# Inverse roots by log and exp on ScalarE, the softmax maximum subtracted on VectorE, and new engine orders in a six-layer local transformer

## The chip, the cores and the metric

The program runs on one core of one Trainium2 chip. The metric is the device time of one execution in microseconds (us); lower is better. PE is TensorE, PEld its weight loads, DVE VectorE, ACT ScalarE, POOL GpSimd, SP SyncE.

## The reference, cut to what matters

Sixteen sequences of 256 tokens, 128 wide, in float32, go through a delta-rule mixer and then through six layers of a local transformer. The layers are what the change touches. Per layer and sequence:

```python
qkv = x @ Wqkv                       # 16 heads of 64; half of x is shifted by one token first
q = l2norm(q) * qs;  k = l2norm(k) * ksc      # t / max(norm(t), 1e-12)
q = q*cos*scale + rotate_half(q)*sin*scale    # k the same with 1/scale
sim = q @ k^T * 8, masked to the token's window of 32 and the one before
attn = softmax(sim)
x = x + (attn @ v) @ Wo
mu, var = mean(x), mean((x - mu)**2)          # on x shifted again
xn = (x - mu) / sqrt(var + 1e-5) * g + b
a, gate = split(xn @ W1 + b1)
x = x + (a * gelu(gate)) @ W2 + b2
```

Two things matter below: the 1/sqrt of 64 sums of squares and 2 variances per token (128 x 66 numbers per item), and the softmax over 64 keys, computed as exp(sim - max) divided by its sum.

## The kernel before

normalise_input, delta_mixer and write_output frame the program and stay as they are. The work of interest is local_transformer. It is a software pipeline: pipeline(body) calls each engine's body once per *item* (one sequence in one layer, 96 items, 100 bodies with the ends). In one body five items are in flight at different stages: new (projected and rotated), turn (scaled, transposed, its values projected), att (scored, softmax), out (weighted sum, output projection) and ffn. Each engine has its own list of calls, written by hand, and runs them strictly in that order; engines meet only through counting semaphores (need(engine, semaphore, value) is a wait that stands in front of the next instruction).

An item has 8 chunks of queries and keys (128 tokens x 512 columns) and 4 units of scores (half a sequence, half of the heads). The steps and their engines:

- query_key (PE, L1416, three matmuls per chunk) fills the single bank ps_proj. rotate (DVE, L1255 and L1262) writes rot_a and rot_b, add (POOL, L1000) adds them into qk, square (ACT, L1079) and sum_squares (DVE, L1270) give the sums ss. The next query_key waits for square.
- inverse_roots (DVE, L1310, L1313, then newton_rsqrt, L63 to L71, eleven steps on 128 x 66) makes rn from ss. scale (POOL, L1010) multiplies qk by rn; turn_qk (PE, L1451) transposes it; turned_out (ACT, L1090) copies it to qT or kT. spread (PE, L1560), deviate (DVE, L1326) and affine (ACT, L1161) use rn for the layer norm.
- score (PE, L1462 and L1468) fills a bank with mask and products; top (DVE, L1279) takes the negated maximum; shift (PE, L1478) adds it in the same bank by a matmul; exp (ACT, L1111) writes pr; total (DVE, L1287, L1290); norm (POOL, L1019); turn_probs (PE, L1492) transposes into the bank ps_p; probs_out (ACT, L1120) copies it to pT; weigh (PE, L1508) multiplies with the values; heads_taken, turn_heads, heads_out and join_heads (L1535) follow.
- value (PE, L1416) projects values, one quarter at a time, into the same bank ps_p, which it shares with turn_probs; value_out (ACT, L1102) copies a quarter to v. window (SP, L947) then copies v into vw, in the layout that weigh wants: 14 DMAs for the first half of an item, 16 for the second. vw has three slots, so the DMAs of the second half wait for weigh(att,1) of the same body (semaphore valued) and for value_out(turn,3). value_out(turn,0) of the next body overwrites v and so waits until all DMAs of both halves have landed.
- ffn_in (PE, L1576, three parts), gelu (ACT, L1170), hidden (DVE, L1335), ffn_out (PE, L1585), layer_out (DVE, L1343).

ps_p makes this order in each body: value(turn,0), its copy, turn_probs(out,3), its copy probs_out(out,3), value(turn,1), its copy, turn_probs(att,0), and so on.

Of the kernel before, what the change touches and what calls it, by code (L numbers as in the profile page):

```python
# [15 lines left out]
P = 128  # L16
# [15 lines left out]
NPREP = 9  # L32
# [14 lines left out]
NEWTON = 11  # L47

# [754 lines left out]
def local_transformer(nc, stateT, ident, wqkv_d, scales_d, wb_d, par_d, rot_d, mask_d):  # L803
# [8 lines left out]
    with ExitStack() as stack:  # L812
        def sb(name, shape, dt=F32):
# [18 lines left out]
        ident_r = sb("ident_r", [P, P], F32R)  # L832
# [11 lines left out]
        rn_t = sb("rn_t", [P, NNORM + 2])  # L844
        qT = sb("qT", [P, 2, NPAIR, L])
# [4 lines left out]
        negmax = sb("negmax", [P, 2, NPAIR], F32R)  # L850
# [18 lines left out]
            "ss_floored", "rn_steps", "added", "scaled", "turned", "turned_out", "v_projected", "v_out",  # L869
# [97 lines left out]
        def _(pool):  # L967
# [8 lines left out]
            nc.gpsimd.tensor_copy(ident_r[:, :], ident[:, :]).then_inc(S["prepared"], 1)  # L976
# [26 lines left out]
            def scale(x, c):  # L1003

                if not x.there:
                    return
                need(pool, S["rn_steps"], x.u * NEWTON + NEWTON)
# [14 lines left out]
            def body(b):  # L1022
                new, turn, att, out, ffn = b.items
                if turn.there:
                    low_half(new, "added", turn.u * 8 + 7)
                else:
                    low_half(new, "prepared", NPREP)
                add(turn, 7)
                scale(turn, 0)
                scale(turn, 1)  # L1030
                scale(turn, 2)
                add(new, 0)
                add(new, 1)
                norm(out, 3)
                scale(turn, 3)
                add(new, 2)
                norm(att, 0)
                scale(turn, 4)
                add(new, 3)
                scale(turn, 5)  # L1040
                add(new, 4)
                norm(att, 1)
                scale(turn, 6)
# [3 lines left out]
                add(new, 6)  # L1047
# [4 lines left out]
        def _(act):  # L1052
# [52 lines left out]
            def exp(x, k):  # L1105
# [4 lines left out]
                need(act, S["p_turned"], x.u * 4 + (k - 1))  # L1110
                nc.scalar.activation(pr[:, k % 2, :, :].rearrange("p h n -> p (h n)"), ps_s[k % 2][:, :], ACT.Exp)\  # L1111
# [51 lines left out]

            def gelu(x):
# [4 lines left out]
                for c, bank in enumerate((ps_c[:, 0:L], ps_c[:, L:2 * L], ps_g[:, 0:L])):  # L1169
                    nc.scalar.activation(gate[:, c, :], bank, ACT.Gelu, bias=par[:, FCH + c:FCH + c + 1])\  # L1170
                        .then_inc(S["gelu_done"], 1)

            def body(b):
# [4 lines left out]
                if b.switch == 1:  # L1178
# [3 lines left out]
                        .then_inc(S["conv_act"], 1)  # L1182
                if b.switch == -1:
                    convert(b, (4, 5), (S["v_projected"], turn.u * 4))
                exp(out, 3)
                probs_out(out, 2)
                heads_taken(out, 1)
                heads_out(out, 1)
                turned_out(att, 7)
                exp(att, 0)  # L1190
                square(new, 0)
                turned_out(turn, 0)
                affine(ffn)
                heads_taken(out, 2)
# [5 lines left out]
                square(new, 2)  # L1200
                probs_out(out, 3)
                turned_out(turn, 3)
                exp(att, 1)
                value_out(turn, att, 1)
                square(new, 3)
                heads_taken(out, 3)
                probs_out(att, 0)
                heads_out(out, 2)
                exp(att, 2)
                turned_out(turn, 4)  # L1210
                square(new, 4)
                heads_out(out, 3)
                heads_taken(att, 0)
                turned_out(turn, 5)
# [5 lines left out]
                square(new, 5)  # L1220
                shift_state(out)
                square(new, 6)
                square_centred(out)
                probs_out(att, 1)
                heads_out(att, 0)
                square(new, 7)
                turned_out(turn, 6)
                value_out(turn, att, 3)

            pipeline(body)  # L1230

        @block.vector
        def _(dve):
# [39 lines left out]
            def top(x, k):  # L1273

                if not x.there:
                    return
                need(dve, S["scored"], x.u * 4 + (k + 1))
                need(dve, S["shifted"], x.u * 4 + (k - 1))
                nc.vector.tensor_reduce(negmax[:, k % 2, :], ps_s[k % 2][:, :].rearrange("p (h n) -> p h n", h=NPAIR),  # L1279
                                        AX.X, ALU.max, negate=True).then_inc(S["maxed"], 1)  # L1280

# [24 lines left out]
            def inverse_roots(new, out):  # L1306
# [7 lines left out]
                if new.there:  # L1314
                    need(dve, S["ss_floored"], new.u + 1)
                if out.there:
                    need(dve, S["var_eps"], out.u + 1)
                if new.there or out.there:
                    newton_rsqrt(nc, dve, ss[:, :], rn[:, new.q, :], rn_t[:, :], S["rn_steps"], new.u * NEWTON)
# [26 lines left out]
            def body(b):  # L1346
                new, turn, att, out, ffn = b.items
                if b.switch == -2:
# [7 lines left out]
                    need(dve, S["rot_ready"], b.layer + 1)  # L1356
                if b.switch == -1:
                    convert(b, (4, 5), 4)
                rotate(new, 0, 0)
                rotate(new, 0, 1)  # L1360
                top(att, 1)
                deviate(ffn)
                sum_squares(new, 0)
                rotate(new, 1, 0)
                rotate(new, 1, 1)
                total(out, 3)
                rotate(new, 2, 0)
                rotate(new, 2, 1)
                top(att, 2)
                sum_squares(new, 1)  # L1370
                hidden(ffn)
                sum_squares(new, 2)
                total(att, 0)
                rotate(new, 3, 0)
                rotate(new, 3, 1)
                sum_squares(new, 3)
                rotate(new, 4, 0)
                rotate(new, 4, 1)
                layer_out(ffn)
# [6 lines left out]
                total(att, 1)  # L1386
# [3 lines left out]
                total(att, 2)  # L1390
# [398 lines left out]
```

## Time and profile before

| | us |
|---|---|
| runs shown | 4334.82, 4339.76, 4342.02 |
| median | 4339.76 |
| profiled execution | 4339.03 |
| its span, first to last instruction | 4336.7 |
| the 96 items of the transformer, by the start of the first and of the last spread matmul | 873.2 to 4305.5 |

The profile lists an instruction with its start and duration. Matmuls overlap: the next may start before the former's shown end, so what one costs PE is read from start to start. "Idle before" is the time that the engine stood still, with the instruction that ended it. The granted TensorE clock is at its full level through the whole transformer.

### The profile page before, as it was taken

Reading aid. Unit: us, or ns where it says so; the run is one execution under the profiler, and the core shown is the slowest. Engines: PE = TensorE matmul, PEld = TensorE weight load, DVE = VectorE, ACT = ScalarE, POOL = GpSimd, SP = SyncE. Lnnn points to the kernel's source line nnn. Section 1 sums busy time; section 2 is a strip of 40 time slices with the busy share of each in tenths; the row PEclk is TensorE's granted clock in tenths of the full one; section 3 lists DMA queues with packets and bytes.
Section 4 is the critical chain, followed back from the end, with each engine's and each line's share of the span. In section 5 each row is a group of like instructions: output and inputs, shape, how many; then the busy total and the mean of one; then the engine's idle time right before and its main releaser. Section 6 shows DMA issues by size and latency. Waiting matters only on the chain. (4 is left out here: it accounts for less than half of the span.)

```text
span 4336.7 us, 147276 instructions
## 1 busy us (share of the span) xinstructions
PE 3870.3 (89%) x60944; PEld 3124.7 (72%) x60944; DVE 3287.5 (76%) x6184; ACT 2662.9 (61%) x4807; POOL 2311.6 (53%) x2140
## 2 busy tenths in 40 slices
PE   4747652799999999999999999999999999999996
PEld 4635541577787777778778777787777777877775
DVE  4385566788888888888888888888888888888873
ACT  2322211477777777777777677777677776777773
POOL 0000001566666666666666666666666666666661
PEclk9666655799999999999999999999999999999998
DMA  1000000222222222223222222222222222222222
GB/s 58 22 12 12 2 12 24 57 73 57 57 57 67 72 57 57 57 51 84 57 56 58 54 66 72 57 57 57 61 78 57 57 57 55 67 57 56 57 57 59
DMA packets 155311, 231.93 MB, mean 53 GB/s; under 512 B 48144, under 2 KB 58128, under 8 KB 152976
## 3 DMA queue, kind: packets, MB, share of 16 engines
q1 hardware_dynamic: 154640, 222.41, 19.7%
q8 instruction: 492, 8.06, 0.8%
q14 instruction: 179, 1.47, 0.1%
HBM read 29.28 MB, written 4.19 MB: 8 GB/s over the span
## 5 line engine op out<-in xcount | busy, mean ns | idle before, releaser
L1000 POOL TENSOR_TENSOR qk<-rot_a,rot_b 128x512 f32<-128x512 f32 x768 | 985.4, 1283 | 754.0 <-PE bank L1451 535.6
L1010 POOL TENSOR_TENSOR qk<-qk,rn 128x512 f32<-128x512 f32 x768 | 806.0, 1060 | 132.9 <-DVE rn L71 132.9
L1255 DVE TENSOR_TENSOR rot_a<-bank,rot 128x512 f32<-128x512 f32 x768 | 526.4, 685 | 373.6 <-PE bank L1416 363.1
L1079 ACT ACTIVATE sq<-bank 128x512 f32<-128x512 f32 x768 | 463.2, 603 | 418.5 <-DVE rot_b L1262 390.5
L1416 PE MATMUL bank<-w_hi,xs_hi 128*128 128x512 f32 x1152 | 565.5, 491 | 60.2 <-ACT sq L1079 36.1
L1270 DVE TENSOR_REDUCE ss<-sq 128x8 f32<-128x512 f32 x768 | 513.8, 669 | 132.4 <-ACT sq L1079 132.2
L1019 POOL TENSOR_TENSOR pr<-pr,prec 128x512 f32<-128x512 f32 x384 | 400.9, 1044 | 322.0 <-DVE prec L1290 322.0
L1262 DVE TENSOR_TENSOR rot_b<-bank,rot 128x512 f32<-128x512 f32 x768 | 522.3, 680 | 0.0
L1451 PE MATMUL bank<-ident,qk 128*128 128x128 f32 x3072 | 470.3, 276 | 25.4 <-POOL qk L1010 21.8
L1416 PE MATMUL bank<-w_hi,xs_lo 128*128 128x512 f32 x1152 | 459.7, 399 | 0.0
L1416 PE MATMUL bank<-w_lo,xs_hi 128*128 128x512 f32 x1152 | 459.2, 399 | 0.0
L1451 PEld LDWEIGHTS bank<-ident,qk 128*128 128x128 f32 x3072 | 373.1, 141 | 114.4 <-POOL qk L1010 39.5
L1468 PEld LDWEIGHTS bank<-kT,qT 64*32 64x32 f32 x24576 | 362.8, 108 | 88.6 <-issue 88.6
L1468 PE MATMUL bank<-kT,qT 64*32 64x64 f32 x24576 | 425.3, 219 | 0.0
L1508 PE MATMUL bank<-vw,pT 128*32 128x128 f32 x12288 | 417.5, 277 | 1.2 <-ACT pT L1120 1.2
L1508 PEld LDWEIGHTS bank<-vw,pT 128*32 128x32 f32 x12288 | 313.9, 110 | 90.0 <-issue 86.5
L1535 PE MATMUL bank<-oT,wo 128*128 128x256 f32 x1536 | 347.3, 379 | 1.4 <-ACT oT L1137 1.4
L1535 PEld LDWEIGHTS bank<-oT,wo 128*128 128x128 f32 x1536 | 291.4, 190 | 44.7 <-ACT oT L1137 1.8
L1137 ACT ACTIVATE oT<-bank 128x512 f32<-128x512 f32 x384 | 229.7, 598 | 106.5 <-PE bank L1523 101.0
L1416 PEld LDWEIGHTS bank<-w_hi,xs_hi 128*128 128x128 f32 x1152 | 221.0, 192 | 94.3 <-issue 38.2
L1576 PE MATMUL bank<-xn,w 128*128 128x256 f32 x1152 | 282.2, 381 | 5.5 <-ACT xn L1161 3.4
L1102 ACT ACTIVATE v<-bank 128x512 f32<-128x512 f32 x384 | 228.6, 595 | 85.8 <-DMA vw<-v 60.9
(242 smaller groups left out, 7377.3 us busy)
## 6 DMA issues: line engine op xcount, KB each, us to landing
vw<-v SPq DMA_DIRECT2D x2880, 64.0 KB, 2.0
stage<-in_wqkv SPq DMA_DIRECT2D x6, 1536.0 KB, 6.3
stage<-in_wb_all SPq DMA_DIRECT2D x6, 1088.0 KB, 5.4
d_band<-in_band SPq DMA_DIRECT2D x8, 512.0 KB, 5.6
d_xt<-in_x SPq DMA_DIRECT2D x4, 512.0 KB, 4.1
base_scratch<-d_res SPq DMA_DIRECT2D x4, 512.0 KB, 2.8
o_base<-base_scratch SPq DMA_DIRECT2D x1, 2048.0 KB, 8.0
out<-o_base SPq DMA_DIRECT2D x4, 512.0 KB, 3.3
```

The costliest lines, as they stand in the source:

```text
L1000: nc.gpsimd.tensor_tensor(qk[:, c, :], rot_a[:, c % 2, :], rot_b[:, c % 2, :], ALU.add)\
L1010: nc.gpsimd.tensor_tensor(y, y, rn[:, x.q, 8 * c:8 * c + 8].unsqueeze(2).to_broadcast([P, 8, DH]), ALU.mult).then_inc(S["scaled"], 1)
L1019: nc.gpsimd.tensor_tensor(y, y, prec[:, k % 2, :].unsqueeze(2).to_broadcast([P, NPAIR, KEYS]), ALU.mult).then_inc(S["normed"], 1)
L1079: nc.scalar.activation(sq[:, :], ps_proj[:, :], ACT.Square).then_inc(S["squared"], 1)
L1255: nc.vector.tensor_tensor(rot_a[:, c % 2, :].rearrange("p (h d) -> p h d", h=8), ps_proj[:, :].rearrange("p (h d) -> p h d", h=8), cos, AL ...
L1262: nc.vector.tensor_tensor(rot_b[:, c % 2, :].rearrange("p (h a d) -> p h a d", h=8, a=2), y[:, :, ::-1, :], sin, ALU.mult).then_inc(S["rot ...
L1270: nc.vector.tensor_reduce(ss[:, 8 * c:8 * c + 8], sq[:, :].rearrange("p (h d) -> p h d", h=8), AX.X, ALU.add).then_inc(S["summed"], 1)
L1416: mm = nc.tensor.matmul(out[:, :], x[:, q, half * P:(half + 1) * P], w[:, cols:cols + CK], start=n == 0, stop=n == 2)
L1451: mm = nc.tensor.transpose(ps_turn[:, i * P:(i + 1) * P], qk[:, c, i * P:(i + 1) * P], ident[:, :])
L1468: mm = nc.tensor.matmul(bank[w * WIN:(w + 1) * WIN, h * KEYS:(h + 1) * KEYS], qT[rows, x.q, h, q0:q0 + WIN], kT[rows, x.q, h, q0:q0 + KEYS ...
L1508: mm = nc.tensor.matmul(ps_o[w * WIN:(w + 1) * WIN, c * P:(c + 1) * P].rearrange("p (r d) -> p r d", r=2), pT[:, k % 2, c, w * WIN:(w + 1) ...
L1535: mm = nc.tensor.matmul(ps_c[:, 0:L], wo[:, c, :], oT[:, c, :], start=c == 0, stop=c == NPAIR - 1)
```

## The change

- The shift matmul, its float32r identity and its semaphore wait in top go. A new DVE step, shift, adds the negated maximum to the bank and writes pr; exp then runs on pr in place.
- newton_rsqrt goes from the transformer (it stays in the other stages). floors (DVE) is what is left of inverse_roots; roots (ACT) takes Ln of ss into ss_log and Exp of -0.5 times that into rn; polish (DVE) makes one Newton step of three instructions.
- After the Gelus the table set with both Exp and Ln is loaded ahead of its first use (EXP_LN_TABLE).
- The lists of PE, DVE, ACT and POOL are written in another order. SP's is unchanged.

```diff
             def exp(x, k):
                 need(act, S["shifted"], x.u * 4 + (k + 1))
-                need(act, S["p_turned"], x.u * 4 + (k - 1))
-                nc.scalar.activation(pr[:, k % 2, :, :].rearrange("p h n -> p (h n)"), ps_s[k % 2][:, :], ACT.Exp)\
+                y = pr[:, k % 2, :, :].rearrange("p h n -> p (h n)")
+                nc.scalar.activation(y, y, ACT.Exp)\
                     .then_inc(S["exped"], 1)
...
+            def roots(new, out):
+                if new.there:
+                    need(act, S["ss_floored"], new.u + 1)
+                if out.there:
+                    need(act, S["var_eps"], out.u + 1)
+                if not new.there and not out.there:
+                    return
+                nc.scalar.activation(ss_log[:, :], ss[:, :], ACT.Ln).then_inc(S["logged"], 1)
+                need(act, S["logged"], new.u + 1)
+                need(act, S["scaled"], min(new.u - 1, NSEQ * DEPTH) * 8)
+                need(act, S["rstd_spread"], out.u - 1)
+                nc.scalar.activation(rn[:, new.q, :], ss_log[:, :], ACT.Exp, scale=-0.5).then_inc(S["rooted"], 1)
...
                         .then_inc(S["gelu_done"], 1)
+                nc.scalar.preload_act_table_set(EXP_LN_TABLE)
...
+                value_out(turn, att, 0)
                 gelu(ffn)
-                value_out(turn, att, 0)
...
+            def shift(x, k):
+                need(dve, S["maxed"], x.u * 4 + (k + 1))
+                need(dve, S["p_turned"], x.u * 4 + (k - 1))
+                nc.vector.tensor_tensor(pr[:, k % 2, :, :], ps_s[k % 2][:, :].rearrange("p (h n) -> p h n", h=NPAIR),
+                                        negmax[:, k % 2, :].unsqueeze(2).to_broadcast([P, NPAIR, KEYS]), ALU.add)\
+                    .then_inc(S["shifted"], 1)
...
+            def polish(new, out):
+                n, y = new.u * POLISH, rn[:, new.q, :]
+                need(dve, S["rooted"], new.u + 1)
+                nc.vector.tensor_tensor(rn_t[:, :], y, y, ALU.mult).then_inc(S["rn_steps"], 1)
+                need(dve, S["rn_steps"], n + 1)
+                nc.vector.scalar_tensor_tensor(rn_t[:, :], rn_t[:, :], -0.5, ss[:, :], ALU.mult, ALU.mult).then_inc(S["rn_steps"], 1)
+                need(dve, S["rn_steps"], n + 2)
+                nc.vector.scalar_tensor_tensor(y, rn_t[:, :], 1.5, y, ALU.add, ALU.mult).then_inc(S["rn_steps"], 1)
...
-            def shift(x, k):
-                need(pe, S["maxed"], x.u * 4 + (k + 1))
-                nc.tensor.matmul(ps_s[k % 2][:, :].rearrange("p (h n) -> p h n", h=NPAIR), ident_r[:, :],
-                                 negmax[:, k % 2, :].unsqueeze(2).to_broadcast([P, NPAIR, KEYS]),
-                                 start=False, stop=True, skip_group_check=True).then_inc(S["shifted"], 1)
```

The new order at three places. First ACT, in the middle of an ordinary body, around the Gelus of ffn. Before (L1079 is square, L1102 value_out, L1120 probs_out, L1090 turned_out, L1111 exp, L1170 gelu):

```order
L1079 ACTIVATE sq<-bank 128x512 [waits t_summed,t_rotated]
L1170 ACT_TABLE_LOAD
L1170 ACTIVATE gate<-bank,par 128x256 [waits t_c_mm]
L1170 ACTIVATE gate<-bank,par 128x256 x2
L1102 ACTIVATE v<-bank 128x512 [waits t_vw_in0,t_vw_in2,t_v_projected]
L1090 ACTIVATE qT<-bank 128x4x128 [waits t_turned]
L1079 ACTIVATE sq<-bank 128x512 [waits t_summed,t_rotated]
L1120 ACTIVATE pT<-bank 128x512 [waits t_valued,t_p_turned]
L1090 ACTIVATE kT<-bank 128x4x128 [waits t_turned]
L1111 ACT_TABLE_LOAD [waits t_p_turned]
L1111 ACTIVATE pr<-bank 128x512 [waits t_shifted]
```

With the change, the same place (L1082 is square, L1105 value_out, L1187 gelu, L1189 the load ahead, L1123 probs_out):

```order
L1082 ACTIVATE sq<-bank 128x512 [waits t_summed,t_rotated]
L1105 ACTIVATE v<-bank 128x512 [waits t_vw_in0,t_vw_in2,t_v_projected]
L1187 ACT_TABLE_LOAD
L1187 ACTIVATE gate<-bank,par 128x256 [waits t_c_mm]
L1187 ACTIVATE gate<-bank,par 128x256 x2
L1189 ACT_TABLE_LOAD
L1123 ACTIVATE pT<-bank 128x512 [waits t_valued,t_p_turned]
L1082 ACTIVATE sq<-bank 128x512 [waits t_summed,t_rotated]
L1093 ACTIVATE qT<-bank 128x4x128 [waits t_turned]
L1105 ACTIVATE v<-bank 128x512 [waits t_v_projected]
```

The copy of the first value quarter, which waits for the landing of vw (t_vw_in), has moved from behind the Gelus to in front of them, and the second table load from behind probs_out(out,3) to in front of it.

Second PE, at the same place. Before (L1478 is shift, L1576 ffn_in part 2, L1492 turn_probs, L1451 turn_qk, L1416 query_key or value, L1585 ffn_out; a row "x3" is the rest of a group):

```order
L1478 MATMUL bank<-negmax,ident_r 128x512 [waits t_maxed]
L1576 MATMUL bank<-xn,w 128x256 [waits t_gelu_done,t_xn_ready]
L1576 MATMUL bank<-xn,w 128x256
L1492 MATMUL bank<-ident,pr 128x128 [waits t_v_out,t_normed]
L1492 MATMUL bank<-ident,pr 128x128 x3
L1451 MATMUL bank<-ident,qk 128x128 [waits t_turned_out,t_scaled]
L1451 MATMUL bank<-ident,qk 128x128 x3
L1478 MATMUL bank<-negmax,ident_r 128x512 [waits t_maxed]
L1416 MATMUL bank<-w_hi,xs_hi 128x512 [waits t_squared]
...
L1585 MATMUL bank<-gate,w 128x256 [waits t_hid_done]
L1585 MATMUL bank<-gate,w 128x256 x2
L1416 MATMUL bank<-w_hi,xs_hi 128x512 [waits t_p_turned_out]
```

With the change (L1523 is turn_probs, L1607 ffn_in part 2, L1456 value and then query_key, L1539 weigh):

```order
L1523 MATMUL bank<-ident,pr 128x128 [waits t_v_out,t_normed]
L1523 MATMUL bank<-ident,pr 128x128 x3
L1607 MATMUL bank<-xn,w 128x256 [waits t_gelu_done,t_xn_ready]
L1607 MATMUL bank<-xn,w 128x256
L1456 MATMUL bank<-w_hi,xs_hi 128x512 [waits t_p_turned_out]
L1456 MATMUL bank<-w_hi,xs_lo 128x512
L1456 MATMUL bank<-w_lo,xs_hi 128x512
L1456 MATMUL bank<-w_hi,xs_hi 128x512 [waits t_squared]
L1456 MATMUL bank<-w_hi,xs_lo 128x512
L1456 MATMUL bank<-w_lo,xs_hi 128x512
L1539 MATMUL bank<-vw,pT 32x128 [waits t_o_out,t_p_turned_out]
```

ffn_in part 2 has moved behind turn_probs(out,3), value(turn,1) ahead of query_key 3 and of ffn_out, and both shifts are gone.

Third DVE, at the boundary of two bodies, with the change (before, eleven rows L63 to L71 stood between L1313 and rotate; L1339 and L1342 are floors, L1275 and L1282 rotate, L1350 to L1354 polish, L1298 top, L1361 deviate, L1307 shift):

```order
L1339 TENSOR_SCALAR ss<-ss 128x64 [waits t_summed]
L1342 TENSOR_SCALAR ss<-bank 128x2 [waits t_var_done]
L1275 TENSOR_TENSOR rot_a<-bank,rot 128x512 [waits t_added,t_projected]
L1350 TENSOR_TENSOR rn_t<-rn 128x66 [waits t_rooted]
L1352 SCALAR_TENSOR_TENSOR rn_t<-rn_t,ss 128x66 [waits t_rn_steps]
L1354 SCALAR_TENSOR_TENSOR rn<-rn_t,rn 128x66 [waits t_rn_steps]
L1282 TENSOR_TENSOR rot_b<-bank,rot 128x512
L1298 TENSOR_REDUCE negmax<-bank 128x8 [waits t_scored]
L1361 TENSOR_TENSOR xc<-xc,bank 128x256 [waits t_rstd_spread]
L1307 TENSOR_TENSOR pr<-bank,negmax 128x512 [waits t_p_turned,t_maxed]
```

The roots now end inside the first rotate of the next body. On PE the boundary has changed too: weigh(att,1) is followed by score(turn,0), turn_probs(att,2), and in the next body by query_key 0, turn_qk 7, score(att,1) and turn_heads(out,1), which stood elsewhere; value(turn,3)'s copy, value_out(att,3) by the names of the next body, is ACT's first work after high_half there, where before it was the last of the former body.

## Rows read from the trace of the kernel before

**Rows 1.** The page, part 1: busy time, share of the span, instructions.

```profile
PE 3870.3 (89%) x60944; PEld 3124.7 (72%) x60944; DVE 3287.5 (76%) x6184; ACT 2662.9 (61%) x4807; POOL 2311.6 (53%) x2140
```

**Rows 2.** Waits: PE from 1000 to 4300 us, ACT and SP whole span.

```profile
PE bank L1492 <- ACT v L1102: 23.4, 30, 1.8
...
ACT v L1102 <- DMA vw<-v: 60.9, 61, 4.3
...
SPq L54 <- PE bank L1508: 1498.9, 189, 12.6
```

**Rows 3.** All spread matmuls (L1560): duration min/median/max, first and last start.

```profile
L1560 PE MATMUL bank<-ident,rn x384: 274/275/582, 873.2 to 4305.5; 128*128 128x128 f32 x192
```

**Rows 4.** PE's timeline: start us, us, instruction, [idle before <-releaser].

```profile
2034.74 1.08 PE L1508 MATMUL bank<-vw,pT 128*32 128x128 f32 x32
...
2070.43 1.08 PE L1508 MATMUL bank<-vw,pT 128*32 128x128 f32 x32
2071.45 0.48 PE L1478 MATMUL bank<-negmax,ident_r 128*128 128x512 f32 x1
2071.77 0.60 PE L1451 MATMUL bank<-ident,qk 128*128 128x128 f32 x4
2072.20 0.60 PE L1492 MATMUL bank<-ident,pr 128*128 128x128 f32 x4
2072.56 0.46 PE L1478 MATMUL bank<-negmax,ident_r 128*128 128x512 f32 x1
2072.86 0.39 PE L1462 MATMUL bank<-mask,ident_b 128*128 128x512 bf16 x1
...
2074.21 0.66 PE L1523 MATMUL bank<-ident,o_tok 128*128 128x128 f32 x4
2074.62 0.48 PE L1416 MATMUL bank<-w_hi,xs_hi 128*128 128x512 f32 x1
...
2077.45 0.66 PE L1451 MATMUL bank<-ident,qk 128*128 128x128 f32 x4 [0.24 <-POOL qk L1010]
...
2086.13 0.63 PE L1492 MATMUL bank<-ident,pr 128*128 128x128 f32 x4 [0.80 <-ACT v L1102]
...
2087.30 0.41 PE L1416 MATMUL bank<-w_hi,xs_hi 128*128 128x512 f32 x1
...
2088.01 1.46 PE L1585 MATMUL bank<-gate,w 128*128 128x256 f32 x6
2089.11 0.58 PE L1416 MATMUL bank<-w_hi,xs_hi 128*128 128x512 f32 x1
...
2107.20 1.08 PE L1508 MATMUL bank<-vw,pT 128*32 128x128 f32 x32
```

**Rows 5.** ACT's timeline, the stretch around the Gelus, and the next body's copy.

```profile
2080.86 0.60 ACT L1079 ACTIVATE sq<-bank 128x512 f32<-128x512 f32 x1 [0.29 <-DVE rot_b L1262]
2081.48 1.28 ACT L1170 ACT_TABLE_LOAD   x1
2082.77 1.20 ACT L1170 ACTIVATE gate<-bank,par 128x256 f32<-128x256 f32 x3
2085.39 0.60 ACT L1102 ACTIVATE v<-bank 128x512 f32<-128x512 f32 x1 [1.41 <-DMA vw<-v]
...
2120.95 0.60 ACT L1102 ACTIVATE v<-bank 128x512 f32<-128x512 f32 x1 [0.21 <-DMA vw<-v]
```

**Rows 6.** SP's timeline, the second half's DMAs of one item; landing times of line L947.

```profile
2071.62 10.68 SPq L947 DMA_DIRECT2D vw<-v  x16
...
DMA to landing us min/median/max: 1.9/2.0/3.8
```

**Rows 7.** DVE's timeline, the root steps between two bodies: first, longest, and rotate.

```profile
2070.81 0.87 DVE L63 TENSOR_SCALAR rn_t<-ss 128x66 int32<-128x66 int32 x1
...
2073.64 1.32 DVE L67 TENSOR_TENSOR rn_t<-rn 128x66 f32<-128x66 f32 x1
...
2076.20 0.68 DVE L1255 TENSOR_TENSOR rot_a<-bank,rot 128x512 f32<-128x512 f32 x1
```

More of the change, by code:

```diff
@@ L1032, in body @@
                 add(new, 0)
+                norm(out, 3)
                 add(new, 1)
[L1034 removed]
+                norm(att, 0)
+                add(new, 2)
                 scale(turn, 3)
[L1036 to L1037 removed]
                 scale(turn, 4)
+                scale(turn, 5)
                 add(new, 3)
[L1040 removed]
+                scale(turn, 6)
                 add(new, 4)
                 norm(att, 1)
[L1043 removed]
                 add(new, 5)
@@ L1219, in body @@
                         .then_inc(S["conv_act"], 1)
-                square(new, 5)
                 shift_state(out)
                 square(new, 6)
+                probs_out(att, 1)
+                turned_out(turn, 6)
                 square_centred(out)
[L1224 to L1228, printed above, removed]
+            nc.scalar.preload_act_table_set(EXP_LN_TABLE)
             pipeline(body)
@@ L1356, in body @@
                     need(dve, S["rot_ready"], b.layer + 1)
+                rotate(new, 0, 0)
+                polish(turn, ffn)
+                rotate(new, 0, 1)
                 if b.switch == -1:
                     convert(b, (4, 5), 4)
-                rotate(new, 0, 0)
-                rotate(new, 0, 1)
-                top(att, 1)
+                top(att, 0)
                 deviate(ffn)
+                shift(att, 0)
                 sum_squares(new, 0)
@@ L1378, in body @@
                 rotate(new, 4, 1)
+                shift(att, 2)
                 layer_out(ffn)
@@ L1401, in body @@
                 rotate(new, 7, 1)
-                top(turn, 0)
+                top(att, 3)
+                shift(att, 3)
                 sum_squares(new, 7)
-                inverse_roots(new, out)
+                floors(new, out)
             pipeline(body)
@@ L1590, in body @@
                 query_key(b, new, 0)
+                turn_qk(att, 7)
+                score(att, 1)
+                turn_heads(out, 1)
                 weigh(out, 2)
@@ L1593, in body @@
                 turn_qk(turn, 0)
+                query_key(b, new, 1)
+                turn_heads(out, 2)
                 value(b, turn, 0)
-                query_key(b, new, 1)
                 turn_qk(turn, 1)
@@ L1598, in body @@
                 ffn_in(ffn, 1)
+                query_key(b, new, 2)
                 turn_qk(turn, 2)
-                query_key(b, new, 2)
                 score(att, 2)
-                shift(att, 1)
+                turn_probs(out, 3, turn, 0)
                 ffn_in(ffn, 2)
-                turn_probs(out, 3, turn, 0)
-                turn_qk(turn, 3)
-                shift(att, 2)
-                query_key(b, new, 3)
-                ffn_out(ffn)
-                value(b, turn, 1)
-                weigh(out, 3)
-                turn_heads(out, 2)
-                turn_probs(att, 0, turn, 1)
+                value(b, turn, 1)
+                query_key(b, new, 3)
+                weigh(out, 3)
+                turn_probs(att, 0, turn, 1)
+                ffn_out(ffn)
+                turn_qk(turn, 3)
+                turn_heads(out, 3)
                 query_key(b, new, 4)
@@ L1615, in body @@
                 weigh(att, 0)
-                turn_heads(out, 3)
+                turn_qk(turn, 5)
                 value(b, turn, 2)
-                turn_qk(turn, 5)
                 query_key(b, new, 5)
@@ L1627, in body @@
                 mean(out)
+                turn_qk(turn, 6)
+                query_key(b, new, 7)
+                value(b, turn, 3)
                 turn_heads(att, 0)
-                query_key(b, new, 7)
-                score(turn, 0)
-                value(b, turn, 3)
-                turn_qk(turn, 6)
                 variance(out)
                 weigh(att, 1)
-                shift(att, 3)
-                turn_qk(turn, 7)
+                score(turn, 0)
                 turn_probs(att, 2, turn, 3)
-                shift(turn, 0)
-                score(turn, 1)
-                turn_heads(att, 1)
             pipeline(body)
```

96 lines of the change are left out of this document (50 added, 46 removed).

## Prediction

> **What bounds the kernel now.** The page comes first: TensorE (PE) is 89% busy over the span, and it is the only engine near full [rows 1]. The list of waits inside the transformer comes second. PE's longest wait there is turn_probs (L1492) for ScalarE's copy of the value projection (value_out, L1102), and that copy in turn waits for the DMAs vw<-v. SyncE issues those DMAs and waits, 189 times, for weigh (L1508) [rows 2]. So PE's own stream is the bound, and behind it, nearly as long, stands one ring: weigh on PE, 16 DMAs, a copy on ScalarE, PE again. I read that ring closely, because the change moves two of its members.
>
> A body (one turn of the pipeline, one item) takes (4305.5 - 873.2) / 95 = 36.13 us on average [rows 3]. Let T0 be the end of weigh(att,1). Undisturbed, T0 to T0 is 2070.43 - 2034.74 = 35.69 us; in the next body it is 2107.20 - 2070.43 = 36.77 [rows 4]. The difference is 0.80 us of wait at turn_probs and 0.24 at a transpose.
>
> **The ring before.** T0 = 2070.43 + 1.08 = 2071.51 [rows 4]. SyncE issues at 2071.62, 16 DMAs in 10.68 us, about 0.6 each, so the last starts near 2081.7; it lands 2.0 us later at the median, 3.8 at most [rows 6]. The earliest landing is therefore T0 + 12.2. The copy starts at V = 2085.39 - 2071.51 = T0 + 13.88 after 1.41 us of waiting; in the next body at 2120.95 - 2108.28 = T0 + 12.67 after 0.21 [rows 4, 5]. ScalarE was free at T0 + 12.46 in both. Over the run it waited 61 times, 60.9 us [rows 2], so V was 12.46 + 1.00 = 13.46 in 61 bodies and between 12.2 and 12.46 in the other 35: I take 12.3 there and a mean V of 13.04. From V to turn_probs is 0.74, from there to the next T0 22.15: 13.88 + 0.74 + 22.15 = 36.77, the disturbed body exactly.
>
> **Part 1: the shift matmul leaves PE.** Four per body. From start to start they take 0.32 (2071.45 to 2071.77) and 0.30 (2072.56 to 2072.86) [rows 4], and I take 1.24 us per body; PE's stream falls to 34.45. Their shown duration, 0.48 and 0.46, overlaps the next matmul. The Trainium skill (Perfetto Trace Analysis, Identifying the Most-Contended Engine) calls matmul busy time a bad measure since matmuls are pipelined; by busy time the gain would read 1.9 us per body, and the trace agrees with the skill.
>
> **Part 2: VectorE.** It gains four 128x512 passes from PSUM, each like rotate's (0.68 us) [rows 7], 2.7 us. It loses eight of eleven root steps: the eleven took 2076.20 - 2070.81 = 5.39 us, three remain, between 0.8 us (0.26 each) and 3.9 (if each is held as long as the longest step, 1.32 [rows 7]). The balance is between -1.9 and +1.2 us on an engine with 76% [rows 1]: no bound.
>
> **Part 3: roots on ScalarE.** Two 128x66 activations, for which there is no row; a 128x512 one takes 0.60, so 0.1 to 0.6 each, likely 0.3. They stand behind heads_taken(out,1), which waits for T0, and the polish stands behind rotate(new,0,0). I get roots done near T0 + 2.4, that rotate near T0 + 3.4, polish near T0 + 4.2 (with long steps T0 + 7.3), against T0 + 4.7 now (2076.20) [rows 7]. PE asks for it in spread, near T0 + 5.8. A delay of 1.5 us there would fall inside the stall of part 4, so this costs nothing. The listed order shows two table loads per body, as before: Ln and all Exps run under the one set that is loaded after the Gelus.
>
> **Part 4: the ring after.** ScalarE now does value_out(turn,0) *before* gelu(ffn); before, after it. SyncE's order and the wait for all 16 DMAs are unchanged. Queued behind the waiting copy are now the Gelu table load, three Gelus, the load of the other set, and probs_out(out,3). And PE has moved too: value(turn,1) must wait for probs_out(out,3), as before, but ffn_in(ffn,2), which needs the second Gelu, now comes behind turn_probs. From V on [rows 5]: copy to the load 0.62 (as 2080.86 to 2081.48), load 1.29 (to 2082.77), Gelus 1.21, second load 1.29, probs_out 0.62, wake-up of PE 0.14 (2085.39 + 0.60 to 2086.13) [rows 4, 5]: 5.17 us until value(turn,1) starts. From there to T0: before, 2108.28 - 2089.11 = 19.17. The new order has query_key 3 (2087.30 to 2088.01, 0.71), ffn_out (to 2089.11, 1.10) and one turn_qk (0.43) more in this stretch, and one turn_heads (0.41) and one score (1.35) less [rows 4]: 19.65 us. The ring is V + 24.82 us. PE alone would reach value(turn,1) at 34.45 - 19.65 = T0 + 14.80; the ring lets it start at 13.04 + 5.17 = T0 + 18.21. So 3.4 us of stall per body take the place of the 1.24 us saved.
>
> I followed the other queues along this order with the same durations. Behind value(turn,1) the tightest is the single projection bank (project, two rotates, square: about 3.3 us per chunk against 4.2 between query_key 3 and 4); it has some 0.6 us to spare. GpSimd's adds are late by nothing that PE asks for.
>
> **Sum.** 13.04 + 24.82 = 37.86 us against 36.13, +1.73 x 95 = +164 us. Off this comes what the layer changes hide: 23.4 us of PE's wait for the copy [rows 2] over the 91 bodies between 1000 and 4300 us are 0.26 each, so an ordinary body is 35.69 + 0.26 = 35.95 and (36.13 - 35.95) x 95 = 17 us belong to conversions at layer changes, most of which will lie under the wait for the landing. 4339.0 (the profiled execution, 2.3 more than its span, 0.7 under the median 4339.8) + 164 - 17 = 4486 us.
>
> **Rivals.** (A) Faster: the landing does not hold the copy and PE's stream sets the time. A body is then 34.45 + 0.18: -1.50 x 95 = -143, 4196 us. It needs V below 34.45 - 24.82 = T0 + 9.6; the gain begins below 36.13 - 24.82 = T0 + 11.3. Against it: 16 issues alone take 10.7. For it: no row shows this ring with the new ScalarE order, and I may have misjudged what stands behind the copy. Chance 0.10.
> (B) V near T0 + 11.3, 4340 us: 0.04.
> (C) Slower still: the DMAs start late. Their first needs value_out(att,3) too, which now stands behind high_half in the next body; I get it done at T0 - 0.2. If square_centred, the transposes or the wait for centre push it 1 us past T0, each body is 1 us longer: 4580 us. Chance 0.07.
> (D) Slower, by the table loads. The rows give 1.29 us from a load to the next activation [rows 5], and the sum goes by them; if a load held the engine twice as long on this path, two loads would add 2.6 us per body, 4730 us. Chance 0.02. The Trainium skill (ScalarE: Activation LUTs, What ACT_TABLE_LOAD costs) puts a switch at 2.66 us with the drain; the trace does not agree.
> That the roots or the shift would not be as the diff says I exclude: the listed orders show them.
>
> **How the numbers follow.** The forecast has 0.77. Its own range: with V = 12.2 throughout the body is 37.02, +0.89 x 95 = +85, with 17 to 35 us off 4390; with V 0.5 us later 4535. Range 4385 to 4535; A, B, most of C and D (about 0.2) lie outside. A comparison of this kernel can tell 0.2%, some 9 us, from no change. Faster 0.10, same 0.04, slower 0.86.
>
> **What would show it.** Right: ScalarE's v copy waits 2 to 4 us for vw<-v in nearly every body; the Gelu load starts 0.6 us after it; PE waits at ffn_in (L1607) for the gate about 1.8 us and at value (L1456) for pT about 1.4; T0 to T0 is 37 to 38.5 us; PE's busy share falls though no other engine rises. Wrong: the copy lands before T0 + 11.3, or PE's stalls lie elsewhere (spread, score), or bodies of 34.5 us.

## The result and the profile after

| | before | after |
|---|---|---|
| median, us | 4338.72 (4334.82 to 4342.02) | 4621.19 (4616.26 to 4635.49) |
| ratio to before | | 1.0657 (95% interval 1.063 to 1.0684) |
| profiled execution, us | 4339.03 | 4625.48 |

The kernel is 6.6% slower. The direction was forecast, the size was not: 4625.5 against 4486, and above the range's 4535. The profile says first that no engine took over.

The page, busy time and the granted TensorE clock in 40 slices of the span, answers to [rows 1]:

```profile
PE 3962.5 (86%) x60560; PEld 3173.1 (69%) x60560; DVE 3143.7 (68%) x5776; ACT 2754.4 (60%) x5009; POOL 2296.7 (50%) x2139
...
PEclk9666656999999999999999999999999999999998
```

PE has 384 matmuls fewer and 92 us more busy time, which already says that its instructions became longer. The digit 9 stands for 90% or more and hides a part of the answer; the stretch from 1600 to 2200 us shows it (length, then PE, PEld, DVE, ACT and POOL busy with instruction counts, granted clock, DMA share, GB/s), before first, after second:

```profile
1600.00:2200.00 600.00, 585.27 (x8755) 473.05 (x8745) 485.48 (x928) 428.59 (x780) 392.77 (x363) 1.00 0.24 61
```

```profile
1600.00:2200.00 600.00, 555.81 (x8044) 444.87 (x8043) 426.32 (x797) 408.24 (x751) 358.11 (x333) 0.94 0.23 57
```

Next the spread matmuls of after, as in [rows 3]:

```profile
L1591 PE MATMUL bank<-ident,rn x384: 274/276/583, 867.9 to 4590.3; 128*128 128x128 f32 x192
```

A body takes (4590.3 - 867.9) / 95 = 39.18 us against 36.13, and 3.05 x 95 = 290 us is the whole difference, 4625.5 - 4339.0 = 286.5, within 4 us. So only the transformer's bodies matter.

The waits of after from 1000 to 4500 us (total us, times, longest), as in [rows 2]:

```profile
ACT v L1105 <- DMA vw<-v: 243.2, 83, 4.2
...
PE bank L1607 <- ACT gate L1187: 119.7, 83, 1.5
...
PE bank L1523 <- ACT v L1105: 59.2, 50, 2.0
...
PE bank L1456 <- ACT pT L1123: 46.8, 59, 1.1
```

ScalarE's copy now waits for the landing in 83 bodies, 2.9 us each, and PE has three stalls in the place of one: turn_probs for the copy, ffn_in part 2 for the Gelu, value(turn,1) for probs_out. One body on ScalarE, with T0 = 2050.66 (weigh at 2049.58 plus its 1.08 us), as in [rows 5]:

```profile
2052.90 0.26 ACT L1175 ACTIVATE ss_log<-ss 128x66 f32<-128x66 f32 x1 [0.34 <-DVE ss L1342]
2053.19 0.26 ACT L1179 ACTIVATE rn<-ss_log 128x66 f32<-128x66 f32 x1
...
2064.76 0.60 ACT L1105 ACTIVATE v<-bank 128x512 f32<-128x512 f32 x1 [3.70 <-DMA vw<-v]
2065.37 1.28 ACT L1187 ACT_TABLE_LOAD   x1
2066.67 1.20 ACT L1187 ACTIVATE gate<-bank,par 128x256 f32<-128x256 f32 x3
2067.89 1.28 ACT L1189 ACT_TABLE_LOAD   x1
2069.18 0.60 ACT L1123 ACTIVATE pT<-bank 128x512 f32<-128x512 f32 x1
```

And on PE, the same body and then the next one (T0 = 2090.09), as in [rows 4]:

```profile
2049.58 1.08 PE L1539 MATMUL bank<-vw,pT 128*32 128x128 f32 x32
...
2065.50 0.63 PE L1523 MATMUL bank<-ident,pr 128*128 128x128 f32 x4 [1.45 <-ACT v L1105]
2067.65 1.87 PE L1607 MATMUL bank<-xn,w 128*128 128x256 f32 x4 [1.52 <-ACT gate L1187]
2069.83 0.79 PE L1456 MATMUL bank<-w_hi,xs_hi 128*128 128x512 f32 x1 [0.32 <-ACT pT L1123]
...
2108.99 0.79 PE L1456 MATMUL bank<-w_hi,xs_hi 128*128 128x512 f32 x1
2109.58 0.63 PE L1456 MATMUL bank<-w_hi,xs_lo 128*128 128x512 f32 x1
2110.01 0.63 PE L1456 MATMUL bank<-w_lo,xs_hi 128*128 128x512 f32 x1
2110.44 0.63 PE L1456 MATMUL bank<-w_hi,xs_hi 128*128 128x512 f32 x1
...
2118.66 0.39 PE L1456 MATMUL bank<-w_hi,xs_lo 128*128 128x512 f32 x1
2118.89 0.39 PE L1456 MATMUL bank<-w_lo,xs_hi 128*128 128x512 f32 x1
```

The chain is that of the prediction, with V = 2064.76 - 2050.66 = T0 + 14.10 and 5.07 us from V to value(turn,1). New is what comes then. Behind the stalls the starts of equal 128x512 matmuls lie 0.43 us apart (2109.58 to 2110.01), nine microseconds later 0.23 (2118.66 to 2118.89): PE runs at the lower of its two clocks, 1.2 instead of 2.4 GHz, for a few microseconds in most bodies. The Trainium skill (TensorE: Matmul & The Clock Gate, Back-to-back issue gap) gives N / 1.2 ns for a cold matmul, which at 512 columns is 427 ns, and the trace agrees with its 0.43 us.

The trace of before holds the same thing, in four places before its last bodies. At each of its five layer changes PE stalls 1.84 us. Behind four of these stalls the clock falls (behind the last, at 3638.03, and behind one of 2.56 us that follows it at 3646.22, it does not), so the clock is not at its full level through the whole transformer, as was said above. The first of them:

```profile
1304.66 0.38 PE L1462 MATMUL bank<-mask,ident_b 128*128 128x512 bf16 x1 [1.84 <-ACT pr L1111]
...
1307.08 0.63 PE L1416 MATMUL bank<-w_hi,xs_lo 128*128 128x512 f32 x1
1307.51 0.63 PE L1416 MATMUL bank<-w_lo,xs_hi 128*128 128x512 f32 x1
```

The spacing is 0.43 us here too. In before it came four times in 96 bodies; with the change it comes in most of them.

I cut each of 93 bodies in after's trace into the terms of the prediction:

| us per body | forecast | after, mean | after, least |
|---|---|---|---|
| V, landing and copy | 13.04 | 13.56 | 12.17 |
| V to value(turn,1) | 5.17 | 5.07 | |
| value(turn,1) to the next T0 | 19.65 | 20.93 | 19.6 in 16 bodies |
| ring | 37.86 | 39.56 | |

At full clock the last term is 19.6, as worked out, but it took 20.1 to 22.4 in 76 of the 93 bodies. In before the same stretch varies by 0.06 us in 92 of 93 bodies; the last body is shorter, in before as in after.

### The profile page after: what moved, and what is told of

Read it like the earlier page. It is cut to its first block and busy times, and to the rows that moved or that the text cites. A ratio compares the mean times of both kernels' runs of the same rounds, so it can differ in the third digit from the quotient of the medians.

```text
span 4623.5 us, 146015 instructions
## 1 busy us (share of the span) xinstructions
PE 3962.5 (86%) x60560; PEld 3173.1 (69%) x60560; DVE 3143.7 (68%) x5776; ACT 2754.4 (60%) x5009; POOL 2296.7 (50%) x2139
## 3 DMA queue, kind: packets, MB, share of 16 engines
q14 instruction: 177, 1.45, 0.1%
## 5 line engine op out<-in xcount | busy, mean ns | idle before, releaser
L1001 POOL TENSOR_TENSOR qk<-rot_a,rot_b 128x512 f32<-128x512 f32 x768 | 985.0, 1283 | 632.8 <-PE bank L1491 589.8
L1011 POOL TENSOR_TENSOR qk<-qk,rn 128x512 f32<-128x512 f32 x768 | 792.8, 1047 | 214.7 <-DVE rn L1354 214.7
L1275 DVE TENSOR_TENSOR rot_a<-bank,rot 128x512 f32<-128x512 f32 x768 | 529.7, 690 | 441.4 <-PE bank L1456 420.0
L1456 PE MATMUL bank<-w_hi,xs_hi 128*128 128x512 f32 x1152 | 592.4, 514 | 122.9 <-ACT pT L1123 50.4
L1082 ACT ACTIVATE sq<-bank 128x512 f32<-128x512 f32 x768 | 456.4, 594 | 285.4 <-DVE rot_b L1282 285.4
L1282 DVE TENSOR_TENSOR rot_b<-bank,rot 128x512 f32<-128x512 f32 x768 | 522.7, 681 | 0.0
L1456 PE MATMUL bank<-w_hi,xs_lo 128*128 128x512 f32 x1152 | 492.2, 427 | 0.0
L1456 PE MATMUL bank<-w_lo,xs_hi 128*128 128x512 f32 x1152 | 491.8, 427 | 0.0
L1539 PE MATMUL bank<-vw,pT 128*32 128x128 f32 x12288 | 451.4, 292 | 1.8 <-ACT pT L1123 1.8
L1607 PE MATMUL bank<-xn,w 128*128 128x256 f32 x1152 | 334.1, 432 | 133.6 <-ACT gate L1187 128.1
L1105 ACT ACTIVATE v<-bank 128x512 f32<-128x512 f32 x384 | 229.4, 597 | 329.4 <-DMA vw<-v 267.2
L1539 PEld LDWEIGHTS bank<-vw,pT 128*32 128x32 f32 x12288 | 338.6, 117 | 93.4 <-issue 84.7
L1456 PEld LDWEIGHTS bank<-w_hi,xs_hi 128*128 128x128 f32 x1152 | 238.9, 207 | 212.4 <-ACT pT L1123 110.5
L1307 DVE TENSOR_TENSOR pr<-bank,negmax 128x512 f32<-128x512 f32 x384 | 263.6, 687 | 127.9 <-PE bank L1523 124.3
L1607 PEld LDWEIGHTS bank<-xn,w 128*128 128x128 f32 x1152 | 225.5, 210 | 181.1 <-issue 148.6
```

Source lines behind the costliest of these rows:

```text
L1001: nc.gpsimd.tensor_tensor(qk[:, c, :], rot_a[:, c % 2, :], rot_b[:, c % 2, :], ALU.add)\
L1082: nc.scalar.activation(sq[:, :], ps_proj[:, :], ACT.Square).then_inc(S["squared"], 1)
L1275: nc.vector.tensor_tensor(rot_a[:, c % 2, :].rearrange("p (h d) -> p h d", h=8), ps_proj[:, :].rearrange("p (h d) -> p h d", h=8), cos, AL ...
L1282: nc.vector.tensor_tensor(rot_b[:, c % 2, :].rearrange("p (h a d) -> p h a d", h=8, a=2), y[:, :, ::-1, :], sin, ALU.mult).then_inc(S["rot ...
L1456: mm = nc.tensor.matmul(out[:, :], x[:, q, half * P:(half + 1) * P], w[:, cols:cols + CK], start=n == 0, stop=n == 2)
L1539: mm = nc.tensor.matmul(ps_o[w * WIN:(w + 1) * WIN, c * P:(c + 1) * P].rearrange("p (r d) -> p r d", r=2), pT[:, k % 2, c, w * WIN:(w + 1) ...
```

## The experiments

Each kernel was timed side by side with the kernel before, on one chip; ratios are to before with their 95% interval. That was done in four groups, in which before had a median of 4338.7 (after), 4334.7 (e1, e2, e3, b2), 4334.6 (d1, d2, e6, e7) and 4332.2 us (e9, b3), so a difference between groups carries up to 6 us of this. "From after" and so on says which kernel was edited. The terms are means over some 93 bodies of a trace, layer changes among them and without the end bodies, so that a body reads 0.2 to 0.4 us more than by the spread matmuls.

| kernel | median us | ratio | V | V to value(turn,1) | to T0 | body |
|---|---|---|---|---|---|---|
| before | 4338.7 | 1 | 13.36 | | | 36.36 |
| after | 4621.2 | 1.0657 [1.063, 1.0684] | 13.56 | 5.07 | 20.93 | 39.56 |
| e1_copy_behind_gelu | 4407.3 | 1.0169 [1.0152, 1.0186] | 14.70 | 2.30 | 20.21 | 37.20 |
| e2_load_late | 4255.8 | 0.9813 [0.9793, 0.9833] | 13.82 | 2.14 | 19.68 | 35.64 |
| e3_filler | 4520.3 | 1.0424 [1.0407, 1.0442] | 13.55 | 5.23 | 19.60 | 38.39 |
| b2_copy_first | 4698.1 | 1.0829 [1.0802, 1.0857] | 13.05 | | | 40.19 |
| d1_twelve | 4245.2 | 0.9788 [0.9769, 0.9808] | 10.90 | 5.08 | 19.6 | 35.57 |
| d2_late_twelve | 4178.7 | 0.9641 [0.9625, 0.9657] | 13.21 | 2.06 | 19.6 | 34.85 |
| e6_pool_four | 4260.1 | 0.9826 [0.981, 0.9843] | 11.06 | 5.08 | 19.6 | 35.71 |
| e7_pool_two | 4182.9 | 0.9651 [0.9635, 0.9667] | 13.22 | 2.07 | 19.6 | 34.89 |
| e9_newton_back | 4235.4 | 0.9773 [0.9756, 0.9791] | 13.71 | 2.10 | 19.6 | 35.39 |
| b3_pool_two | 4326.6 | 0.9985 [0.9975, 0.9994] | 12.93 | | | 36.30 |

My theory after reading the two traces was the ring of the prediction with a tail stretched by the lower clock. The main rivals were that the lost time comes from the new PE order or from the new steps themselves. The few long bodies at the layer changes raise the means of V; in an ordinary body V is 12.80 in d2 and e7.

**e1_copy_behind_gelu**, from after: the copy goes back behind the Gelus on ScalarE.

```diff
-                value_out(turn, att, 0)
                 gelu(ffn)
+                value_out(turn, att, 0)
```

> The changed kernel with one pair of calls on ScalarE swapped back: gelu (with the load behind it) first, then value_out(turn,0). Theory (the copy that waits for the landing holds the Gelus and both table loads, and PE behind them): ScalarE is free at T0 + 10.4, loads and Gelus end at T0 + 14.2, the copy, turn_probs, probs_out and value(turn,1) follow at T0 + 16.4, a body is about 36.0 to 36.4 us, and the time 4320 to 4370 us; the copy waits for the landing in few bodies. Rival (the rest of the new orders, or the roots on ScalarE, cost the time): within 1% of the changed kernel, 4575 to 4665 us.

Measured 4407.3, above what was expected. One swap of two calls takes back 214 of 282 us, so the order on ScalarE is the cause of most of it. But with the swap alone both table loads stand in front of the copy, which waits for the landing only 9 times between 1000 and 4300 us (5.4 us in all) and starts at V = 14.70, and the clock is still at 0.97 in 1600 to 2200 us. On PE of e1:

```profile
2061.16 0.84 PE L1523 MATMUL bank<-ident,pr 128*128 128x128 f32 x4 [1.58 <-ACT v L1105]
...
2063.93 0.63 PE L1456 MATMUL bank<-w_hi,xs_lo 128*128 128x512 f32 x1
2064.35 0.63 PE L1456 MATMUL bank<-w_lo,xs_hi 128*128 128x512 f32 x1
```

A single stall of 1.58 us and the spacing is 0.42 again. Such a stall, 1.57 us or more, stands in each of e1's 93 bodies, yet in 38 of them, some with 1.9 us, the tail keeps its 19.6 us: the length of the stall alone does not tell whether the clock falls.

**e2_load_late**, from e1: the load of the second table set moves from behind the Gelus further down ScalarE's list, to just ahead of the next Exp.

```diff
-                nc.scalar.preload_act_table_set(EXP_LN_TABLE)
...
+                if ffn.there:
+                    nc.scalar.preload_act_table_set(EXP_LN_TABLE)
```

> As the run before it (Gelus ahead of the copy), and the load of the Exp and Ln set moved from behind the Gelus to just before exp(att,1). Theory: the copy starts at the landing or at T0 + 12.9, whichever is later, value(turn,1) some 2.1 us after it, a body is 35.1 to 35.7 us, the time 4230 to 4300 us, below the kernel before. Rival (the landing alone sets the body, whatever stands behind the copy): no faster than the run before it.

4255.8, as expected and 1.9% faster than before (the interval, 0.9793 to 0.9833, leaves no doubt of the gain). V falls to 13.82, the tail to 19.68, and the clock is back at 0.99. The load cost 1.3 us of ScalarE time in both kernels; only its place in the ring made it cost (37.20 - 35.64) x 95 = 148 us.

**e3_filler**, from after, output unchanged: 14 extra matmuls per body, into a bank that is free, stand at the three places where PE stalls, so that PE works there instead of waiting.

```diff
+                filler(out, 3)
                 turn_probs(out, 3, turn, 0)
+                filler(out, 7)
                 ffn_in(ffn, 2)
+                filler(out, 4)
                 value(b, turn, 1)
```

> The changed kernel with 14 idle matmuls per body on PE (128x512 bf16, constants, into a bank that is free then) placed in its three stalls: 3 ahead of turn_probs(out,3), 7 ahead of ffn_in part 2, 4 ahead of value(turn,1); 3.2 us of work more per body, output unchanged. Theory (after its stalls PE works at the lower granted clock, which lengthens the stretch from value(turn,1) to T0 from 19.6 to 20.9 us): with the stalls filled that stretch is 19.6 to 19.9 us, the granted clock is 1.00 in the transformer, and the time falls by 80 to 130 us, to 4490 to 4540 us, although PE does more. Rival (the stretch is long for waits, not for the clock): the time stays within 0.5% of the changed kernel or rises.

4520.3, as expected: 101 us *faster* than after with 1344 matmuls more. The stretch from 1600 to 2200 us in its trace:

```profile
1600.00:2200.00 600.00, 588.20 (x8407) 459.52 (x8406) 435.96 (x815) 418.50 (x767) 368.29 (x343) 0.99 0.23 58
```

The granted clock is 0.99 where after has 0.94. V stays, the second term grows by 0.16 us for the fillers, and the tail is 19.60: full clock was worth 20.93 - 19.60 = 1.33 us per body, 126 us, less 15 for the fillers. This is the part that the prediction lacked.

**b2_copy_first**, from before: the same swap, the other way round, and nothing else of the change.

```diff
-                gelu(ffn)
                 value_out(turn, att, 0)
+                gelu(ffn)
```

> The kernel before with only this one pair of calls on ScalarE swapped, value_out(turn,0) ahead of gelu; nothing else of the change. Theory: in this kernel's PE order ffn_in part 2 stands ahead of turn_probs, so value(turn,1) comes 6.7 us after the copy and a body is 13.4 + 6.7 + 19.2 = 39.3 us at full clock, 39.5 to 40.5 with the clock lowered after the stalls: 4660 to 4760 us, slower than the whole change. Rival (the cost comes from the other parts): within 1% of the kernel before.

4698.1, as expected. The swap alone makes the old kernel 8.3% slower, more than the whole change does. The wait that costs PE most in it, from 1000 to 4300 us:

```profile
PE bank L1576 <- ACT gate L1170: 218.2, 77, 4.2
```

In the old order PE asks for the Gelu before turn_probs, so it stands 2.8 us there. The new steps and the rest of the new order are therefore not needed to get the loss; in the new PE order, which asks for the Gelu behind turn_probs, the swap costs less: V to value(turn,1) is 6.5 us in b2 and 5.07 in after.

**d1_twelve**, from after: four of the 16 DMAs of a half are left out (part of vw then keeps older values), so the landing comes some 2.4 us earlier. A measurement of V's worth.

```diff
-HALF_DMAS = (14, 16)
+HALF_DMAS = (14, 12)
...
-                            if n >= 0:
+                            if n >= 0 and not (half == 1 and r == 1 and a == 1):
```

> The changed kernel without 4 of the 16 DMAs of an item's second half (the current window's values of one head group stay zero in vw, so that part of the attention output is left out); nothing else moves. Theory (a body is the landing V plus 5.07 us on ScalarE plus PE's stretch to T0): 4 issues of 0.59 us less bring V from T0 + 13.6 to about T0 + 11.2, ScalarE waits 0.5 to 1.0 us instead of 2.8, the stretch is 19.6 to 20.3 us, a body 35.9 to 36.6 us, the time 4310 to 4390 us. Rival (the landing is not what starts the copy, or the clock stays low whatever the stall): above 4500 us.

4245.2, below what was expected. V fell by 2.66 us, about the four issues (4 x 0.59) and a little more, and the tail by another 1.33, since the stall in front of turn_probs is gone and the clock stays up (0.99). What is left on PE, from 1000 to 4100 us:

```profile
PE bank L1456 <- ACT pT L1123: 63.0, 87, 1.1
```

0.7 us once a body, and behind it no fall of the clock. From after to d1 the landing gave 2.66 us and the body 3.99, so each microsecond of landing had been paid one and a half times.

**d2_late_twelve**, from e2: the same four DMAs left out.

> The kernel with the Gelus ahead of the copy and the late table load, without the same 4 DMAs (the same part of the output is left out). Theory: the landing is now before ScalarE is free at T0 + 12.8 in nearly all bodies, so PE's own stream sets the body at 34.4 to 34.7 us, that is the 1.24 us per body that the shift matmuls cost and no more, with the clock at 1.00: 4140 to 4185 us. Rival (DVE, ScalarE or GpSimd is the next bound): bodies stay above 35.2 us and the time above 4220 us.

4178.7. An ordinary body takes 34.45 us, exactly the 34.45 that the prediction gave to PE's stream. This is the floor of the order with the landing hidden. Against d1, the copy and the table load in the wrong place still cost 0.72 us a body.

**e6_pool_four**, from after, with a complete output: the four DMAs are issued by GpSimd in place of SP (window_tail, on a semaphore of its own that value_out and weigh wait for too).

```diff
+            def window_tail(x):
...
+                need(pool, S["v_out"], x.u * 4 + 4)
+                need(pool, S["valued"], x.u * 4 - 2)
+                for w in range(0, 4):
+                    nc.gpsimd.dma_start(vw[KEYS + WIN:P, slot(x, 1), w, 1, :], v[w * WIN:(w + 1) * WIN, 1, CK:2 * CK])\
+                        .then_inc(S["vw_pool"], 16)
```

> The changed kernel with the same 4 DMAs issued by GpSimd, behind its first add of a body and ahead of scale(turn,0); nothing left out. Theory: as the run with twelve, V near T0 + 11.2 and 4310 to 4390 us, if GpSimd's four issues end before PE needs the scaled chunk (about 2 us free there); what they take there has no row, and if it is 1 us or more each, PE waits for scale and the time is 4390 to 4480 us.

4260.1, again better than expected and for the reason of d1. With all bytes sent V is 11.06, with four DMAs left out it was 10.90: what had held the landing back was not bytes but SP's issue time. GpSimd takes 0.50 us for each:

```profile
2070.78 2.00 POOL L1002 DMA_DIRECT2D vw<-v  x4
```

The Trainium skill (DMA: Bandwidth & Descriptors, Issuing engines are not separate DMA queues) says that issuing from several engines saves only the time that the sequencer takes to initiate, "which is usually small relative to the DMA itself". That time is what it saved here. One issue, 0.59 us, is also small beside one landing, 2.0 us, as the page says; but 16 of them stand one behind another, 10.7 us and more, ahead of the last landing, and so are the larger part of V.

**e7_pool_two**, from e2: two of the 16 on GpSimd.

> The kernel with the Gelus ahead of the copy and the late table load, with 2 of the 16 DMAs issued by GpSimd; nothing left out. Theory: V falls by 1.2 us, most landings come before ScalarE is free, bodies of 34.6 to 35.0 us, 4170 to 4215 us. Rival: GpSimd's issues delay scale(turn,0) by more than the 1.5 us to spare, and PE waits there instead: 4240 us or more.

4182.9, 3.5% faster than before, and the best kernel with a complete output. The copy waits for the landing once between 1000 and 4100 us:

```profile
ACT v L1117 <- DMA vw<-v: 1.5, 1, 1.5
```

**e9_newton_back**, from e7: the roots go back to VectorE.

```diff
-                roots(turn, ffn)
...
-                polish(turn, ffn)
...
+                    newton_rsqrt(nc, dve, ss[:, :], rn[:, new.q, :], rn_t[:, :], S["rn_steps"], new.u * NEWTON)
```

> This is the fastest kernel so far (late landing, copy behind the gelu, two of the sixteen DMAs of a turn issued by GpSimd, 4183 us) with one part of the change undone: the inverse roots are again the eleven short steps of VectorE instead of log, exp and one Newton step. Theory one, the roots on ScalarE are worth something once the landing is out of the way: the roots are then ready near T0+6.9 instead of near T0+4, the rotation and the squares of the first chunk wait for them, and TensorE stands still 2 to 3 us more in each body: 4370 to 4470 us, and more if the granted clock drops as well. Rival: the eleven steps are hidden by other work, as they seemed to be in the kernel before, and the time is within 0.5% of 4183 us.

4235.4: neither. The roots on ScalarE are worth 52 us, not 187 and more, and not nothing. DVE of e9, T0 = 3702.17, and GpSimd beside it:

```profile
3704.43 0.26 DVE L65 TENSOR_SCALAR rn_t<-ss 128x66 int32<-128x66 int32 x1
...
3707.19 0.68 DVE L1287 TENSOR_TENSOR rot_a<-bank,rot 128x512 f32<-128x512 f32 x1
```

```profile
3702.93 1.27 POOL L1011 TENSOR_TENSOR qk<-rot_a,rot_b 128x512 f32<-128x512 f32 x1
3704.15 1.03 POOL L1002 DMA_DIRECT2D vw<-v  x2
3707.36 1.05 POOL L1021 TENSOR_TENSOR qk<-qk,rn 128x512 f32<-128x512 f32 x1 [2.18 <-DVE rn L73]
```

The eleven steps took 2.76 us here and 5.39 in before [rows 7]; I had expected the latter. In before GpSimd's two-input steps run beside each long one (its add L1000 started at 2073.60, and the step of 1.32 us at 2073.64); here it issues DMAs or waits. The Trainium skill (SBUF — State Buffer, SBUF: two separate sides) describes a port pair that VectorE, in some of its steps, and GpSimd hold against each other for a whole instruction, and the two traces agree with it. The later rotate delays the square and by it the projection bank: ordinary bodies are 34.73 against 34.47 us, 25 us in all. The rest, some 25, lies at the layer changes: from 1000 to 4100 us PE waits for w_lo 33.7 us in five waits, against 14.4 in e7, and for oT at ffn_in 10.1 us against 2.3.

**b3_pool_two**, from before: two DMAs on GpSimd and nothing else.

> This is the kernel before with one edit: two of the sixteen DMAs of a turn are issued by GpSimd instead of SP. Theory: the wait of TensorE for the landing in the kernel before (some 0.4 us per body, the difference of its 36.1 us and 35.7 us of its other work) goes and TensorE alone sets the body: 4305 to 4320 us, so that the other parts of the change are worth some 120 us against 4183 us with the landing out of the way. Rival: the landing binds nothing in the kernel before, and it is unchanged within 0.2% (4326 to 4343 us).

4326.6, a gain of 0.15%. This lies outside the theory's 4305 to 4320 and just inside the rival's range, but not for the rival's reason, that the landing binds nothing. PE's wait for the copy does go (0.6 us over 1000 to 4200, 21.7 in before), and an ordinary body is 35.70. But PE's waits for scale and square grew:

```profile
PE bank L1463 <- POOL qk L1020: 24.4, 77, 2.1
PE bank L1428 <- ACT sq L1090: 19.9, 10, 3.1
```

Together they were 28.4 us in before, so 16 of the 21 us were given back. GpSimd's issues stand between its add and its scale, and the body's mean is 36.04 by the spread matmuls. So the landing was worth little before the change, and with it removed in both, the change is worth 4326.6 to 4182.9, 3.3%: 52 us for the roots, 91 for the shift matmul with the order (e9 against b3). No run separates these two; by PE's stream the four shift matmuls alone are 1.24 x 95 = 118 us.

## Why the prediction was right and wrong

- **What bounds, and the ring**: right. V to value(turn,1) is 5.07 for 5.17, the least V is 12.17 for 12.2, the copy waits 2.9 us in 83 bodies, and the Gelu load starts 0.61 us behind it. PE waits at the two places named, for the Gelu 1.4 us (forecast 1.8) and for pT 0.8 us in 59 bodies (forecast 1.4), and at one that was not named as a stall, turn_probs, 1.2 us in 50 bodies. d2's 34.45 fits the price of the shift matmul, 1.24 us. T0 to T0 was to be 37 to 38.5 us and is 39.56, for the two reasons that follow.
- **The tail term, 19.65 us**: this is the step that failed. It was read in bodies of before in which PE does not stall for long, at full clock, and used for bodies in which PE stalls 1.5 us twice in a row. It is 19.6 at full clock and 20.93 on the mean: 1.28 x 95 = +122 us. e3 removed just this. The prediction held a row with a stall of 0.80 [rows 4], after which the clock stays; I took that as leave to keep the clock out of the sum and gave it no rival, though the same trace shows the fall behind stalls of 1.84 us at its layer changes. With the measured 1.28 the sum would be 4608.
- **Mean V, 13.04**: mis-sized by 0.52, +49 us. I worked it out from the copy's waits alone and took 12.3 for the bodies without one. Cut body by body, before's own mean is 13.36: its 31 bodies without a wait have 13.4 on the mean, since at the layer changes ScalarE comes late (up to 16.8). In after it is the landing itself: 88 of 93 bodies wait for it, to a mean V of 13.4, and five at layer changes have 16.3. SP's 16 issues took 10.68 us in the body that I read, 10.0 to 12.9 us over the bodies of before (mean 10.98), and 11.26 us on the mean in after, so one reading set the floor but not the mean. What makes some issues long stays open.
- **The credit of 17 us for layer changes**: 39.56 - 39.18 is 36 us over 95 bodies, but some of it is the end bodies. Together the misses are 122 (tail) + 49 (V) - 9 (the second term) - 19 (this credit) = 143 us, against the 139 by which the sum was too low.
- **Parts 2 and 3**: roots took 0.26 us each for an estimated 0.3, were done at T0 + 2.8 for 2.4, and the steps of polish 0.22 to 0.23 each; no stall of PE in after stands at spread, so they cost nothing there, and e9 shows that they gain 52 us once the ring is open.
- **Rivals**: A's threshold holds. d1 with V = 10.90 should take 35.7 by V + 24.82 and takes 35.57, and the kernel is then faster. C and D did not occur: the first DMA is issued 0.11 us behind T0, and a load takes 1.29 us to the next activation.

## What to carry over

In an in-order engine queue, a step that waits for a landing has to stand behind everything that another engine asks for sooner; one swap of two calls cost the old kernel 8.3% here, and in the new one hid changes worth 3.3%. When a forecast puts new stalls on TensorE, cost the work behind them at both clocks. When many small DMAs end a ring, count issue time before bytes, and let another queue issue two of them.

## What the runs showed of the hardware

- PE's clock fell to the lower level behind stalls of 1.45 and 1.52 us in one body of after, behind single stalls of 1.57 us and more in 55 of e1's 93 bodies (not in the other 38), and behind four of the five of 1.84 us in before (not behind the fifth, nor behind one of 2.56). It didn't behind the single ones of before's ordinary bodies, 0.80 us in the one shown and 1.79 at most, nor behind d1's of 0.7 us on the mean. What decides it between these lengths stays open. Filling the stalls with useless matmuls kept it at the higher level and made the kernel 101 us faster.
- One of the vw<-v DMAs takes SP 0.59 us to issue at the median and GpSimd 0.50 (e6) to 0.52 (e7), and GpSimd's next step waits for that.
- A table load costs 1.29 us of ScalarE's queue (2065.37 to 2066.67 in after is 1.30). The Trainium skill (ScalarE: Activation LUTs, What ACT_TABLE_LOAD costs) gives some 1283 ns for the load, which the trace bears out with 1.28 us, and 2.66 us with a drain, which no load here shows.
- Eleven dependent 128x66 steps on VectorE take 2.76 us with GpSimd issuing DMAs or waiting (e9) and 5.39 beside GpSimd's two-input steps (before).
